# Row maxima stored in query order and read with step one, and the diagonal mask of the row maxima moved to a TensorE matmul

## What the reference computes

```
k, q, v = per-head projections of xn            # 16 heads, 2048 x 128 each
scores  = q k^T, causal mask, softmax(scores / sqrt(128))
z       = attn v ;  s = W_O z
g       = silu(xn W_base + b + routed low-rank term)
out     = x + s * g
```

## Time and profile before

| | |
|---|---|
| time, median of 3 runs | 1548.5 us (1548.2 to 1549.68) |
| the profiled execution's own time | 1548.1 us |
| its span in the profile | 1546.2 us |
| TensorE busy | 94% of the span |
| VectorE busy | 81% |
| ScalarE busy | 82% |
| GpSimd busy | 51% |
| mean granted TensorE clock | 0.989 |

### The profile page before, as it was taken

How to read it: one execution, slowest core, us unless ns; L and a number is a source line. 1 busy time by engine, 2 the same in 40 slices (tenths; PEclk the granted TensorE clock), 3 DMA queues, 4 the chain that set the end, 5 groups by cost and what they waited for, 6 DMA issues and landing times.

```text
span 1546.2 us, 23204 instructions
## 1 busy us (share of the span) xinstructions
PE 1459.5 (94%) x7788; PEld 1193.2 (77%) x7788; DVE 1248.1 (81%) x2541; ACT 1274.0 (82%) x2196; POOL 793.4 (51%) x688
## 2 busy tenths in 40 slices
PE   5999999999999999999999999999999999999997
PEld 4877778777877878777787777877787777877765
DVE  6788877888788886888868887788878898788864
ACT  2788898889888898898988888888987988888962
POOL 2444655455465555456554555554645555544740
PEclk9899999999999999999999999999999999999998
DMA  2100010000100001000010001000010000100002
GB/s 75 49 8 14 15 25 25 15 15 8 29 21 15 15 7 42 15 14 13 10 42 15 7 15 28 22 15 14 8 35 21 15 7 13 40 8 15 15 28 82
DMA packets 30070, 33.75 MB, mean 22 GB/s; under 512 B 11008, under 2 KB 17664, under 8 KB 29952
## 3 DMA queue, kind: packets, MB, share of 16 engines
q1 hardware_dynamic: 29952, 32.26, 8.3%
HBM read 30.02 MB, written 2.23 MB: 21 GB/s over the span
## 4 chain that ended last, share of the span: by engine, by line
PE 51%; ACT 24%; DVE 13%; issue 9%; POOL 2%; DMA 0%; SPq 0%; ACTq 0%; POOLq 0%; DVEq 0%
PE ps L281 15%; PE ps L282 14%; PE ps L283 14%; ACT ps L478 7%; ACT probs L498 7%; ACT p_hi L499 6%; DVE p_lo L551 6%; PE ps L719 4%; DVE partmax L566 3%; POOL colsum L433 2%; PE ps L754 2%; ACT qT_hi L486 1%; DVE z_lo L588 1%; ACT z_hi L504 1%; PE ps L731 1%
## 5 line engine op out<-in xcount | busy, mean ns | idle before, releaser
L433 POOL TENSOR_TENSOR colsum<-colsum,probs 128x512 f32<-128x512 f32 (+3 forms) x512 | 610.2, 1192 | 388.3 <-ACT probs L498 373.6
L478 ACT ACTIVATE ps<-maxrow 128x512 f32<-128x512 f32 (+3 forms) x640 | 645.3, 1008 | 8.9 <-DMA maxrow<-max_dram 8.7
L551 DVE TENSOR_TENSOR p_lo<-probs,p_hi 128x512 fp32r<-128x512 f32 (+3 forms) x640 | 614.9, 968 | 42.4 <-ACT p_hi L499 41.4
L498 ACT ACTIVATE probs<-ps 128x512 f32<-128x512 f32 (+3 forms) x640 | 362.9, 567 | 141.4 <-PE ps L731 74.8
L499 ACT ACTIVATE p_hi<-ps 128x512 fp32r<-128x512 f32 (+3 forms) x640 | 365.3, 571 | 0.0
L566 DVE TENSOR_REDUCE partmax<-ps 128x1 f32<-128x512 f32 x384 | 256.9, 679 | 10.4 <-PE ps L719 9.5
L281 PE MATMUL ps<-qT_hi,kT_hi 128*128 128x512 f32 (+3 forms) x640 | 247.6, 387 | 12.7 <-ACT ps L478 9.6
L281 PE MATMUL ps<-p_hi,v_hi 128*128 128x512 f32 (+3 forms) x640 | 241.7, 378 | 13.2 <-DVE p_lo L551 12.2
L282 PE MATMUL ps<-qT_lo,kT_hi 128*128 128x512 f32 (+3 forms) x640 | 234.3, 366 | 0.0
L283 PE MATMUL ps<-qT_hi,kT_lo 128*128 128x512 f32 (+3 forms) x640 | 233.9, 366 | 0.0
L282 PE MATMUL ps<-p_lo,v_hi 128*128 128x512 f32 (+3 forms) x640 | 233.5, 365 | 0.0
(11 more groups left out here) (106 smaller groups left out, 2174.8 us busy)
## 6 DMA issues: line engine op xcount, KB each, us to landing
maxrow<-max_dram SPq DMA_DIRECT2D x64, 256.0 KB, 3.8
wraw<-wqk_dram SPq DMA_DIRECT2D x16, 256.0 KB, 3.8
acc<-x_dram SPq DMA_DIRECT2D x4, 512.0 KB, 7.2
wraw<-wv_dram SPq DMA_DIRECT2D x8, 256.0 KB, 4.7
wraw<-wo_dram SPq DMA_DIRECT2D x8, 256.0 KB, 2.9
probs<-x_dram SPq DMA_DIRECT2D x4, 512.0 KB, 4.5
out_dram<-acc SPq DMA_DIRECT2D x4, 512.0 KB, 3.0
max_dram<-rowmax SPq DMA_DIRECT2D x64, 2.0 KB, 1.4
```

What stands on the lines that cost most here:

```text
L433: nc.gpsimd.tensor_tensor(total[:, c0:], total[:, c0:], tile[:, c0:], ALU.add)\
L478: nc.scalar.activation(st[job.n % SCORE_BANKS].rearrange("p (t n) -> p t n", t=TB)[:, q:, :], maxrow[:, job.g, :].rearrange("p (n t) -> p ...
L498: nc.scalar.activation(probs[:, k, c0:], src, ACT.Exp, scale=SCALE).then_inc(probs_ready, 1)
L551: nc.vector.tensor_tensor(p_lo[:, k, c0:], probs[:, k, c0:], f32(p_hi[:, k, c0:]), ALU.subtract)\
```

## The change

The store writes query t*128+p to place t*128+p, four bytes at a time; the seed reads `maxrow` straight with step one. On the diagonal block the matmul of a row maximum is followed by a second one, which adds the mask to its last 128 columns in the same bank, and VectorE takes a plain maximum. `mask_rows`, `wait_slot`, the memset and the masked copy in SBUF are gone.

```
@@ constants, buffers
-        mask_rows = sb("mask_rows", [P, BW])
-        wait_slot = sb("wait_slot", [P, AUX_BANKS])
-        masked_row = gate[:, :, :, :].rearrange("p a t d -> p (a t d)")[:, 0:AUX_BANKS * BW]\
-            .rearrange("p (k n) -> p k n", k=AUX_BANKS)
@@ SyncE, the store of a block's maxima
-                    sp.dma_start(row.rearrange("(p t) -> p t", t=TB), rowmax[:, job.g, :]).then_inc(max_out, 16)
+                    sp.dma_start(row.rearrange("(t p) -> p t", p=P), rowmax[:, job.g, :],
+                                 allow_slow_non_contiguous=True).then_inc(max_out, 16)
@@ GpSimd, start
-            nc.gpsimd.memset(mask_rows[:, :], 0.0).then_inc(made, 1)
-            nc.gpsimd.affine_select(out=mask_rows[:, BW - P:], in_=mask_rows[:, BW - P:], compare_op=ALU.is_ge,
-                                    fill=MASKED, base=0, pattern=[[-1, P]], channel_multiplier=1)
@@ ScalarE, seed
-                q = columns(job) // P
-                nc.scalar.activation(st[job.n % SCORE_BANKS].rearrange("p (t n) -> p t n", t=TB)[:, q:, :],
-                                     maxrow[:, job.g, :].rearrange("p (n t) -> p t n", t=TB)[:, q:, :],
-                                     ACT.Copy, scale=-1.0).then_inc(seeded, 1)
+                c0 = columns(job)
+                nc.scalar.activation(st[job.n % SCORE_BANKS][:, c0:], maxrow[:, job.g, c0:], ACT.Copy, scale=-1.0)\
+                  .then_inc(seeded, 1)
@@ VectorE, RowMax
-                    if job.c < job.g:
-                        nc.vector.reduce_max(dst, src, axis=AX).then_inc(aux_free, 1)
-                    else:
-                        w = P * (job.q + 1)
-                        k = job.aux % AUX_BANKS
-                        nc.vector.memset(wait_slot[:, k:k + 1], 0.0)
-                        nc.vector.tensor_tensor_reduce(
-                            out=masked_row[:, k, 0:w], in0=src[:, 0:w], in1=mask_rows[:, BW - w:], scale=1.0,
-                            scalar=-3.0e38, op0=ALU.add, op1=ALU.max, accum_out=dst).then_inc(aux_free, 1)
+                    w = P * (job.q + 1) if job.c == job.g else BW
+                    nc.vector.reduce_max(dst, src[:, 0:w], axis=AX).then_inc(aux_free, 1)
@@ TensorE, RowMax
-                    nc.tensor.matmul(dst[:, 0:w], qT_hi[:, job.g, job.q * P:(job.q + 1) * P],
-                                     kT_hi[:, k_slot(job.head, job.c), 0:w], start=True, stop=True)\
-                      .then_inc(aux_full, 1)
+                    op = nc.tensor.matmul(dst[:, 0:w], qT_hi[:, job.g, job.q * P:(job.q + 1) * P],
+                                          kT_hi[:, k_slot(job.head, job.c), 0:w], start=True, stop=job.c < job.g)
+                    if job.c == job.g:
+                        op = nc.tensor.matmul(dst[:, w - P:w], mask_bf[:, :], ident_bf[:, :], start=False, stop=True)
+                    op.then_inc(aux_full, 1)
```

More of the change, by code:

```diff
@@ L398, in _ @@
                 nc.gpsimd.memset(rank[:, :, e:e + 1], float(E - e))
-            pool.wait_ge(made, 5)
+            pool.wait_ge(made, 4)
             diagonal = dict(compare_op=ALU.not_equal, base=0, pattern=[[-1, P]], channel_multiplier=1)
```

## The result

The changed kernel takes 1788.8 us (1782.4 to 1793.4) against 1548.35: 1.155 times the time before, 95% interval 1.151 to 1.159. It is slower by 240 us, far outside the range given.

The account below looks back on a forecast made before the run. TensorE, 94% busy, was nearly full and lost 105 us to ScalarE and VectorE in turn. 1548.1 - 34 (seeds) - 32 (VectorE) + 31 (masks) - 1 (start) = 1512, forecast 1513, own range 1498 to 1530, range with rivals 1490 to 1544.

Parts of the forecast that it names:

- the store's term: Store of row maxima on SyncE: 4-byte pieces add 0.2 to 0.6 us, at most 1.9; up to 0.6 costs nothing.
- The Trainium skill's rule that the prediction weighed: Store's DMA: below 512 bytes an engine reads, modifies and writes; no other sum unless 4 bytes are worse than 16.
- the store lands late: Rival, chance 0.06: store 4 us later delays the load behind it and the block's first seed, 35 us lost, 1548.
- a seed's wait for the load of the maxima beyond 20 us in all: Sign on ScalarE's seeds: the forecast is wrong if their wait for that load grows beyond 20 us in all.
- cover: Slack between load of maxima, first seed and TensorE's score: 1.2 us in eight tightest blocks, 1.7 with the shorter seed.
- break-even: Store landing 4 us later, at 5.5 us, was put at 1548 us; from there on the kernel is slower.
- The seed's term: ScalarE's seeds at step one: 659 ns for 512 columns, 303 for 128, 270 us less of ScalarE's 1253.
- What the seed would free: TensorE's 105 lost us: 34 of the seeds' 39 and 32 of VectorE's 66 were expected back.
- The half of VectorE's waits that was kept: Of TensorE's 66 us lost to VectorE, about half, 32, would go, as VectorE's own waits are for ScalarE.
- VectorE's waits for hi parts halved: Sign of success: VectorE's waits for ScalarE's hi parts, 64.3 us for v alone and 220 with others, halve.
- The masks' term: Added mask matmuls on TensorE: 256 at 0.12 us, 31 us in all, bounds 10 and 59.
- VectorE and the start: VectorE sheds accumulator reads and memsets, 15 us taken (bounds 0 and 35); the start gives 1 us back.

Follow-up runs that it names:

- the run with 4.0 us more: Masks-and-seed kernel (changed kernel with the old store) plus two extra stores of 512 spaced 4-byte pieces ahead of each block's own: 1569.5 us.
- 2.0 us (1486): Masks-and-seed kernel (changed kernel with the old store) plus one extra store of 512 spaced 4-byte pieces ahead of each block's own: 1486.1 us.
- a kernel at 1476: Changed kernel with the old 16-byte store put back, masks on TensorE and step-one seed kept: 1476.3 us.
- seed alone: Kernel before with only the seed's reading changed to step one, old store, masks on VectorE: 1448.8 us.
- store-and-seed alone: Kernel before with the 4-byte store and step-one seed, masked maximum left on VectorE: 1796.9 us.
- the version with masks on VectorE: Kernel before with step-one seed and maxima turned by VectorE, stored in 128-byte pieces; masked maximum left on VectorE: 1446.2 us.
- the turned store: Changed kernel with VectorE turning the maxima in 32 by 32 blocks, stored as 16 pieces of 128 bytes in four transfers: 1475.0 us.

## Why the prediction was wrong

- **The step that failed is the store's term.** "At 32 pieces for an engine instead of 8 that is 0.2 us more by packet time, and up to 0.6 if their spread over time grows by four", with an upper bound of 1.9. Measured: 7.0 us more in the kernel (8.4 against 1.4 in the median), with a load behind it that lands 1.0 later than before, and up to 8.6 more alone. The price was taken from what packets take, and from the slowest landing of a store whose pieces are 16 bytes, four to a stretch of 64. The changed kernel's own row shows how far packet time misleads; the 528 packets of one store, in 40 slices from 422.4 to 430.8, are all recorded within slices 5 to 7, that is by 1.5 us, and the landing comes some 7 us after them:

```profile
DMA  0000281000000000000000000000000000000000
```

  The right row would have had pieces side by side of less than 16 bytes, and the trace before has none. The case should have had bounds as open as that, and a larger chance than 0.06. The Trainium skill's rule that the prediction weighed (DMA: Bandwidth & Descriptors, Specifications: below 512 bytes a read-modify-write) doesn't tell these stores apart: 128 pieces of 4 bytes take 1.4 us at a distance of 16 bytes and 7.3 side by side. Whether it holds here, no run shows.
- **The rival "the store lands late" is what happened**, by the mechanism that it names (load, first seed, TensorE), and the prediction's own sign, a seed's wait for the load of the maxima beyond 20 us in all, came at 285. Its cover was read too wide. For 4 us more it counted 35 us of loss; the run with 4.0 us more lost 93 (in its profiled execution 101, of which 62 are idle time and 39 busy time at a slower clock), and the prediction gave the clock no price. So the break-even is nearer than its 4 us: between 2.0 us (1486) and 4.0 us (1569) a straight line crosses 1548 at about 3.5, and that from a kernel at 1476 and not at 1513. Beyond it, 7.1 us gave 312, of which 98 are longer busy time at the slower clock.
- **The seed's term was right.** 0.66 us was worked out for 512 columns and 0.30 for 128; measured 0.61 and 0.29. The 128-column seed is a single run of elements in both kernels and still fell from 427 to 290 ns, so it is the step and not the number of runs in the access. The two pages of the Trainium skill that the prediction weighed come out so. ScalarE: Activation LUTs (What ACT_TABLE_LOAD costs) had 0.61, as measured. Of SBUF — State Buffer (Door 1: The DMA port swizzle) the crossing of a line agrees with the measurement and "a step of 4 fp32 is free" does not: that step more than doubled the seed's cost per element, from 0.84 to 1.90 ns.
- **What the seed would free was mis-sized.** 66 of TensorE's 105 lost us were expected back; seed alone gave 99. The half of VectorE's waits that was kept (34 us) went with the long seeds too. The prediction's reason, that VectorE waits for ScalarE's hi parts and for v's above all, is not borne out in that form: the waits for v stayed (64.3 and 61.9 us), so the sign "VectorE's waits for hi parts halved" did not come true even in the seed-alone kernel.
- **The masks' term was right in size where TensorE is full.** 31 us were counted; 27.5 and 28.8 measured there, 5 to 6 where it still waits. Between the changed kernel and store-and-seed alone they cost nothing (1788.8 and 1796.9). The distance start to start of the earlier trace rows was the right measure.
- **VectorE and the start** are too small to be told apart. That moving the maximum off the masked form freed VectorE bought nothing: the version with masks on VectorE is the fastest.

## What to carry to other kernels

Price a store by its landing and by how its pieces lie in memory: pieces shorter than 16 bytes side by side took 3 to 10 us, and longer or more distant ones mostly 1.4 to 2.7. When one of several engines feeds the others in order, waits recorded at a second engine may belong to it: relieving ScalarE took away VectorE's share as well. And a pause of some microseconds in TensorE is paid beyond its own length: behind the 5.8 us shown above the clock was 0.50 for some 5 us. Last, an added delay must be read from its own run: a store that took 2.6 us by itself took 2.0 in the kernel.

## What was not expected of the hardware

512 pieces of 4 bytes 64 bytes apart (2.7 us) and 512 bytes apart (1.8) land faster than 128 pieces side by side (7.2 to 9.0). The time depends on the distance: 7.3, 3.1 and 1.4 us at 4, 8 and 16 bytes. A load of the same 256 KB lands after 3.1 us in the median behind the turned store, 3.8 to 3.9 behind the old one and 4.8 to 5.0 behind the new one. No packet record shows the store's price; only the time to the semaphore does. And an instruction of ScalarE that reads SBUF with a step of 16 bytes took 1155 ns for 512 elements against 613 with step one.
